# Causal attention with fills: TensorE's order laid over two steps, single logits and single fills between whole values

## The reference

```python
mod = (silu(c) @ wmod).reshape(2, 6, 1, 256)
h = layernorm(x) * (1 + ca) + sa                 # x: (2, 2048, 256)
q, k, v = heads(h @ W_qkv.T + b_qkv)             # 16 heads of 16
logits = einsum('bhqd,bhkd->bhqk', q, k) / sqrt(16)
logits = where(causal, logits, -inf)
o = einsum('bhqk,bhkd->bhqd', softmax(logits), v)
x = x + ga * (o @ W_out.T + b_out)
h = layernorm(x) * (1 + cb) + sb
x = x + gb * ffn(h)      # two layers, each with a routed mixture of low-rank terms; relu between
```

## Time and profile before

| | us |
|---|---|
| median of 3 runs (range) | 1361.06 (1353.09 to 1361.54) |
| the profiled execution's own time | 1362.05 |
| its span, first to last instruction | 1360.2 |
| first logits to last values (the attention) | 138.1 to about 1009 |
| PE busy | 1221.2 (90%) |
| DVE busy | 950.9 (70%) |
| ACT busy | 804.3 (59%) |

### The profile page before, as it was taken

The page is one execution under the profiler, slowest core; times in us unless marked ns, Lnnn a source line. Parts: engine busy times, 40 slices in busy tenths (PEclk is TensorE's granted clock), DMA queues, the critical chain, the costliest instruction groups (busy, mean ns, idle before and its releaser), DMA issues.

```text
span 1360.2 us, 23639 instructions
## 1 busy us (share of the span) xinstructions
PE 1221.2 (90%) x9456; PEld 714.0 (52%) x9456; DVE 950.9 (70%) x1247; ACT 804.3 (59%) x1616; POOL 175.7 (13%) x125
## 2 busy tenths in 40 slices
PE   2988889999999999999999999999962999999997
PEld 2875433444444444444444444434322888888886
DVE  7767897888787887787887777865203567666654
ACT  2542366777677777677777667777631544444442
POOL 8003700000111000000000000000003132323211
PEclk9987799999999999999999999999865999999999
DMA  4684130031041021031021021000013011111200
GB/s 154 217 267 175 40 72 10 8 84 35 31 115 47 10 77 37 10 89 40 9 62 52 10 79 49 9 9 11 9 34 123 1 62 49 42 43 55 63 16 32
DMA packets 58118, 79.53 MB, mean 58 GB/s; under 512 B 12680, under 2 KB 28752, under 8 KB 58008
## 3 DMA queue, kind: packets, MB, share of 16 engines
q1 hardware_dynamic: 58008, 78.01, 18.9%
HBM read 47.57 MB, written 29.62 MB: 57 GB/s over the span
## 4 chain that ended last, share of the span: by engine, by line
PE 66%; DVE 16%; ACT 8%; issue 7%; DMA 1%; POOL 1%; SPq 0%; POOLq 0%; ACTq 0%; DVEq 0%
PE ps L829 20%; PE ps L811 17%; PE ps L373 8%; PE ps L791 8%; ACT prob L1011 6%; PE ps L767 5%; PE ps L905 5%; DVE mx L1161 4%; DVE hid_lo L1273 4%; DVE xhat L401 2%; DVE stats L391 1%; ACT o_sb L1002 1%; DVE x L1227 1%; DVE x L1223 1%; DMA rd<-rden_rows 1%
## 5 line engine op out<-in xcount | busy, mean ns | idle before, releaser
L1011 ACT ACTIVATE prob<-ps 128x512 f32<-128x512 f32 (+3 forms) x1280 | 597.7, 535 | 258.1 <-PE ps L767 136.3
L1161 DVE TENSOR_REDUCE mx<-ps 128x2 f32<-128x1024 f32 (+1 forms) x512 | 593.2, 1190 | 171.7 <-PE ps L791 97.6
L811 PE MATMUL ps<-qst,kst 64*128 64x512 f32 (+3 forms) x1280 | 380.9, 448 | 13.1 <-ACT prob L1011 7.3
L811 PEld LDWEIGHTS ps<-qst,kst 64*128 64x128 f32 x1280 | 174.7, 186 | 323.7 <-ACT prob L1011 283.7
L829 PE MATMUL ps<-prob,vw 128*32 128x512 f32 (+3 forms) x2560 | 306.6, 551 | 9.8 <-ACT o_sb L1002 9.8
L791 PE MATMUL ps<-kst,qst 62*128 62x512 f32 (+3 forms) x1280 | 247.7, 417 | 20.9 <-DVE mx L1161 17.7
L791 PEld LDWEIGHTS ps<-kst,qst 62*128 62x128 f32 x1280 | 125.9, 191 | 64.0 <-DVE mx L1161 55.7
L767 PE MATMUL ps<-mask_kh,eye_h 64*128 64x128 bf16 x1024 | 100.6, 225 | 0.0
L829 PEld LDWEIGHTS ps<-prob,vw 128*32 128x32 f32 x2560 | 51.7, 108 | 74.6 <-ACT prob L1011 49.7
L1273 DVE TENSOR_TENSOR hid_lo<-hidf,hid_hi 128x512 fp32r<-128x512 f32 x64 | 73.1, 1182 | 12.8 <-ACT hid_hi L1055 12.7
L905 PE MATMUL ps<-w_hi,hid_hi 128*128 128x284 f32 x256 | 78.6, 328 | 2.0 <-ACT hid_hi L1055 2.0
(11 more groups left out here) (150 smaller groups left out, 1402.8 us busy)
## 6 DMA issues: line engine op xcount, KB each, us to landing
qk_parts<-parts SPq DMA_DIRECT2D x32, 512.0 KB, 4.2
qst<-qk_parts SPq DMA_DIRECT2D x192, 64.0 KB, 2.3
kst<-qk_parts SPq DMA_DIRECT2D x192, 64.0 KB, 2.3
xs<-in_x SPq DMA_DIRECT2D x16, 512.0 KB, 7.2
o_all<-o_sb SPq DMA_DIRECT2D x32, 256.0 KB
o_raw<-o_all SPq DMA_DIRECT2D x16, 256.0 KB
rd<-rden_rows SPq DMA_DIRECT2D x16, 256.0 KB
out<-y SPq DMA_DIRECT2D x8, 512.0 KB, 3.1
```

The lines of the kernel that those rows point to most:

```text
L811: last = pe.matmul(ps[:, banks[par], 0:BLK - skip], kst[g % 2][rows, pair, t * P:(t + 1) * P], qst[g % 2][rows, pair, J * BLK + skip:(J + ...
L1011: act.activation(prob[:, n % P_BUFS, h, 0:width], ps[:, L_BANK + i % L_BUFS, 0:width], ACT.Exp).then_inc(exp_done, 1)
L1161: dve.tensor_reduce(mx[:, u % 2, :, pairs[0], r, cb], ps[:, bank:bank + 2, 0:width], AX, ALU.max).then_inc(max_red, 1)
```

## The change

PE's order is now written for two steps at a time. The fills of both steps stand in one list `es`. `logits` takes single heads, also of two different steps; its masks are set per head (`mask_keys`), and the fills' masks have a function of their own (`mask_queries`) with the same matmuls. `values` is the same. On ACT the copy of a finished unit moves from behind head 1 of the second step after the unit's last to behind head 0 of the third.

```diff
-                for n in range(NS):
+                for n in range(0, NS, 2):
+                    es = [*ORDER[1 + n], *ORDER[2 + n]]
+                    logits((n, 0), (n, 1))
+                    for e in es[0:1]:
+                        fill(e)
+                    logits((n, 2))
+                    for e in es[1:2]:
+                        fill(e)
+                    logits((n, 3), (n + 1, 0))
                     if n >= PV_LAG:
-                        values(n - PV_LAG)
-                    logits(n, 0)
-                    for e in ORDER[1 + n][:2]:
+                        values(n - 2)
+                    logits((n + 1, 1))
+                    for e in es[2:3]:
                         fill(e)
-                    logits(n, 1)
-                    for e in ORDER[1 + n][2:]:
+                    logits((n + 1, 2), (n + 1, 3))
+                    for e in es[3:]:
                         fill(e)
-                for n in range(NS - PV_LAG, NS):
-                    values(n)
+                    if n >= PV_LAG:
+                        values(n - 1)
+                values(NS - 2)
+                values(NS - 1)
...
-                        if h == 1 and n - PV_LAG in UNIT_AT_END:
-                            copy_out(UNIT_AT_END[n - PV_LAG])
+                        if h == 0 and n - PV_LAG - 1 in UNIT_AT_END:
+                            copy_out(UNIT_AT_END[n - PV_LAG - 1])
```

In the new `logits` the wait is the same per head:

```diff
+                def logits(*heads):
+
+                    for n, h in heads:
...
+                        until(pe, exp_done, 4 * n + h - L_BUFS + 1)
+                        rows = slice(h % 2 * STACK, h % 2 * STACK + ROWS + MROWS)
```

More of the change, by code:

```diff
@@ L759, in _, with mask_queries @@
                     project(n)
-                def mask(banks, col, table):
+                def mask_queries(bank, col):
                     for half in range(2):
@@ L766, in mask, with mask_keys @@
                             rows = slice(par * STACK, (par + 1) * STACK)
-                            last = pe.matmul(ps[:, banks[par], col:col + P], eye_h[rows, half, :],
-                                             table[rows, half, :], start=False, stop=True, skip_group_check=True)
-                            if half == 1 and table is mask_kh:
+                            last = pe.matmul(ps[:, bank + par, col:col + P], eye_h[rows, half, :],
+                                             mask_qh[rows, half, :], start=False, stop=True, skip_group_check=True)
+                    return last
+                def mask_keys(heads):
+                    for half in range(2):
+                        for n, h in heads:
+                            rows = slice(h % 2 * STACK, (h % 2 + 1) * STACK)
+                            last = pe.matmul(ps[:, L_BANK + (4 * n + h) % L_BUFS, 0:P], eye_h[rows, half, :],
+                                             mask_kh[rows, half, :], start=False, stop=True, skip_group_check=True)
+                            if half == 1:
                                 last.then_inc(st_done, 1)
-                    return last
                 def fill(e):
@@ L796, in fill @@
                         for at in range(len(pairs)):
-                            last = mask((bank, bank + 1), (at + 1) * width - P, mask_qh)
+                            last = mask_queries(bank, (at + 1) * width - P)
                     last.then_inc(fill_done, 1)
[L800 to L813, removed]
+                def logits(*heads):
+                    for n, h in heads:
+                        u, t = STEPS[n]
+                        g, J = UNITS[u]
+                        skip = skip_of(n)
+                        if n == FIRST[u] and h == 0:
+                            pe.wait_ge(m_in[u % 2], 16 * M_DMAS * (u // 2 + 1))
+                        until(pe, exp_done, 4 * n + h - L_BUFS + 1)
+                        rows = slice(h % 2 * STACK, h % 2 * STACK + ROWS + MROWS)
+                        last = pe.matmul(ps[:, L_BANK + (4 * n + h) % L_BUFS, 0:BLK - skip],
+                                         kst[g % 2][rows, h // 2, t * P:(t + 1) * P],
+                                         qst[g % 2][rows, h // 2, J * BLK + skip:(J + 1) * BLK],
                                          start=True, stop=True)
@@ L816, in logits @@
                             last.then_inc(st_done, 1)
-                    if diagonal(n):
-                        mask(banks, 0, mask_kh)
+                    if diagonal(heads[0][0]):
+                        mask_keys(heads)
                 def values(n):
```

## The result

The changed kernel takes 1367.28 us (median of 15 runs, 1362.16 to 1373.66) against 1361.33 us before (15 runs): ratio 1.0052, 95% interval 1.0032 to 1.0071. It is slower by about 6 us. The forecast was 1384, range 1366 to 1402: the direction held, the size was almost four times too large, and most of the chance lay on a loss that could be told from none by 1%, which this is not.

A forecast was written before the change was run, and what follows sets the result against it. It took a ring of waits between PE and ACT, not a full engine, to bound the attention. Terms by class of step pairs summed to +21.5 us on the profiled 1362.05, forecast 1384 us, range 1366 to 1402.

The forecast's parts named there:

- The ring before: Attention steps before the change: PE's logits and ACT's exponentials wait for each other, 2.67 us per step, two fills free beside.
- The first half, 3.16 us: Heads 0 to 4, then values: 0.60 + 0.49 + 0.65 + 0.43 + 0.99 us to the next logits, hiding two fills.
- The second half, three links of 0.34: Heads 5 to 7 and remaining fills: PE's own chain, 0.34 us each to 1.01, then 0.43 and 0.99, 2.43 us.
- crowded pairs: Pairs of steps with five or more fills: seven inner ones +0.3 us each, five crowded first pairs -0.3 each.
- Masks: Fills with masks in a pair's second half cost 0.4 instead of 0.34 us: +0.15 where both fills have masks.
- rival of the hidden loads: Weight loads hide where single heads leave half the array free: links 0.24 us, -39 us, 1345 us; chance 0.09.
- no change that can be told: Lone head 5 in the second half costs half a slot: -22 us, about 1362 to 1372 us; chance 0.15.
- The copy, +0.47 in second pairs: ACT's copy between exponentials 0 and 1 of a unit's third step delays head 4 by 0.47 us.
- The -0.80 that I had put on first pairs: First two steps of the next unit, with shorter values: 4.54 us instead of 5.34, mostly a shift to the pair behind.
- rival of stalling fills: Last fills of crowded pairs wait for DVE and turns wait, stalling exposed PE: +15 us, 1399 us; chance 0.14.
- The sum: Attention pairs by class: +10.9 inner, +17.3 second, -16.7 first, +6 and +6 masked, -2 four-step units; total +21.5 us.
- 0.62 less a tenth of it, with 0.14: Chance of over 1% slower: the main case's 0.62 less a tenth, plus the worse case's 0.14, given as 0.72.

The follow-up runs named there:

- second pair of profiles: Both kernels, the changed one and the one before, profiled once more unedited: attention 877.6 and 869.3 us, last stage 344.6 and 349.6 us.

## Why the prediction was right and wrong

**The ring before: right.** 2.67 us by 0.60 + 0.65 + 0.43 + 0.99, whatever the fills. The doubled fill in the kernel before cost nothing, and moving values back behind head 3 brought pairs of few fills back to 5.33.

**The first half, 3.16 us: right to 0.01.** Pairs of two fills came to 4.82 (forecast 4.91).

**The second half, three links of 0.34: the step that failed.** The term was "0.34 each until the last fill has started (1.01)". It measured 0.34 + 0.24 + 0.24, and 0.33 rather than 0.43 from the last fill to the values: 2.14 in place of 2.43. With four plain fills that is 5.29 instead of 5.59, a small gain where I had put +0.25. The same term stands in the first pairs of a unit, 4.23 where I had 4.54, and in the second ones. The 133 pairs of up to four fills, for which my terms come to roughly +14 us, took 6 to 8 us less than before. That is a difference of some 20 us, most of it from this term and more than the whole miss of 17; the crowded pairs below gave a part of it back. Masks went the other way: with four masked fills an inner pair takes 0.33 more than with plain ones, where I had 0.15. I had taken 0.34 from the earlier trace rows, and each of those links stands behind values or behind a wait for DVE. That links without a wait are shorter stood in the trace of before as well, for instance here, where two fills take 0.47 together:

```profile
345.15 0.63 PE L791 MATMUL ps<-kst,qst 62*128 62x512 f32 x4
345.62 0.40 PE L811 MATMUL ps<-qst,kst 64*128 64x512 f32 x1
```

Both signs that I had named for being wrong came: links under 0.3, and inner pairs of four plain fills under 5.34.

The rival of the hidden loads had the right number, 0.24 from the earlier trace rows, and I gave it 0.09. Its point of decision was a link of 0.28; one link of 0.34 and two of 0.24 are 0.27 in the mean, so by that rival the loss should have been gone, and in the pairs of up to four fills it is. Its mechanism is not what the runs show: it had the single heads free the array for loads, but the pairs of before (345.15 to 345.62 above) have the same short links. The Trainium skill's gap of 0.216 us for 512 columns (TensorE: Matmul & The Clock Gate, Back-to-back issue gap), which the page calls that of an isolated matmul, is nearer to the running links of 0.23 to 0.24 than my 0.34 was; the first link behind values, 0.34 here, is not covered by it.

The result, 1367, lies in the range of the rival *no change that can be told* (1362 to 1372), and that is luck: it had the lone head 5 cost half a slot, but the head takes a whole link. It is also by luck that the time lies inside my range, by 1 us: the short links, the crowded pairs and a shorter last stage happen to add up so.

**The copy, +0.47 in second pairs: right, but not to be had back.** They came to 5.77, 0.48 over the inner ones, with the copy between exponentials 0 and 1. But with the copy moved ahead they stay at 5.68: the short first pair leaves ACT full. The -0.80 that I had put on first pairs was -1.10, and 0.4 of it came back right behind.

**Crowded pairs: a rival's mechanism, under-priced in my sum.** I had put +0.3 on inner pairs of five fills and a little on others; they took +1.05, and all 27 crowded pairs 16 to 19 us. Spreading them gave 16 us, which is the 15 us that the rival of stalling fills had priced, and I had ruled it mostly out because DVE has room on average. The time of that rival, 1399, was wrong only because it stood on top of my links of 0.34.

**The sum.** By class the attention of the second pair of profiles moved by -24 us in first pairs, +13 in second, +5 in inner, +7 and +3 in the masked, and +3.5 in the units of four steps, +8 in all, against -17, +17, +11, +6, +6 and -2 forecast. Of the 16 fills that I had counted beyond two in pairs of 256 and 128, eight stand in the units of four steps. Why the second pair of such a unit rose from 4.10 to 5.07 stays open. And 0.62 less a tenth of it, with 0.14, is 0.70, not 0.72. The waits also fell short of the forecast: PE's loads still wait 239 us for ACT, because the first half of a pair still waits for exponentials.

## What to carry to other kernels

Read the cost of a slot on a full engine from a stretch where it waits for nothing: a link behind a wait holds start-up that a running chain hides. When a ring is opened on one side, ask what each half ends on: work that was free beside the ring is paid slot by slot, a fill behind the instruction that waits is on the path, and a third fill behind the last head makes the values wait for DVE. A pair of steps that becomes nearly as short as another engine's work in it leaves that engine no idle moment, and any extra work of it (here the copy) shows in the next pair.

## What the runs showed of the hardware

Matmuls of 64 rows and 512 columns at 2.4 GHz, each with new weights, start 0.23 to 0.25 us apart in the same half of the rows once running, whether the halves go in step (345.15 to 345.62 before) or staggered (511.77 to 512.25 after). The first link behind values or a wait is 0.33 to 0.34 us. The values start 0.33 us behind the last of such a chain, and 0.43 behind a matmul that is itself the first behind a wait. A lone matmul in one half does not hold up the other half, but takes a whole link of its own (511.44 to 511.77). And a last stage with unchanged code took 343 to 352 us, with 58 to 80 us of it at 1.2 GHz.
